# Causal attention with split values: two value products a block instead of three, row sums from the exp, and the rope's high parts on GpSimd

## What is computed

```python
q = (xn @ wq)                       # per head: 128 numbers without position, 64 with rope
ckv, k_pe = split(xn @ wkv_a)       # 64 latent numbers, 64 rope numbers, shared by the heads
ckv = ckv * rsqrt(mean(ckv**2) + eps) * kv_norm_scale
k_nope, v = split(ckv @ wkv_b)      # per head
scores = (q_nope . k_nope + rope(q_pe) . rope(k_pe)) * 192 ** -0.5, causal
s = concat_heads(softmax(scores) @ v) @ wo
g = silu(ffn(xn))                   # 256 -> 704 -> 256, ternary weights
out = x + s * g
```

## Time and profile before

| | |
|---|---|
| median of 3 runs | 1092.98 us (1091.6 to 1100.86) |
| the profiled execution | 1093.28 us, its span 1091.5 us |
| mean granted TensorE clock | 0.953 |
| busy of the span: PE / PEld | 971.0 us (89%) / 839.1 us (77%) |
| DVE / ACT / POOL | 739.6 us (68%) / 790.7 us (72%) / 716.4 us (66%) |
| DMA packets | 591978, 170.23 MB |
| the chain that ended last, by engine | PE 36%, POOL 17%, ACT 13%, issue 11%, DVE 8%, DMA 8%, SPq 6% |

### The profile page before, as it was taken

How to read it: one execution, slowest core, us unless ns; L and a number is a source line. 1 busy time by engine, 2 the same in 40 slices (tenths; PEclk the granted TensorE clock), 3 DMA queues, 4 the chain that set the end, 5 groups by cost and what they waited for, 6 DMA issues and landing times.

```text
span 1091.5 us, 26364 instructions
## 1 busy us (share of the span) xinstructions
PE 971.0 (89%) x10560; PEld 839.1 (77%) x10560; DVE 739.6 (68%) x1093; ACT 790.7 (72%) x1157; POOL 716.4 (66%) x514
## 2 busy tenths in 40 slices
PE   5648988999898979998989899979899997889998
PEld 5636877878787868786878787868787786777887
DVE  5747767777777767686778777877767785762134
ACT  1439887888788877888788878887888786663222
POOL 3657867696759685878487848784878576723231
PEclk7879998999999999998999999999989998899999
DMA  5019999999999989999999999998999999992001
GB/s 169 10 49 171 184 171 178 176 181 181 185 170 176 196 165 171 171 178 178 170 182 176 181 180 183 186 179 167 177 175 179 158 177 196 187 168 78 1 20 59
DMA packets 591978, 170.23 MB, mean 156 GB/s; under 512 B 574064, under 2 KB 585968, under 8 KB 591856
## 3 DMA queue, kind: packets, MB, share of 16 engines
...
## 4 chain that ended last, share of the span: by engine, by line
PE 36%; POOL 17%; ACT 13%; issue 11%; DVE 8%; DMA 8%; SPq 6%; ACTq 1%; POOLq 0%; DVEq 0%
PE s_ps L623 14%; PE s_ps L525 9%; POOL hl L1113 8%; ACT hl L729 6%; PE slot_ps L525 5%; POOL pe L1113 4%; ACT prob L806 4%; DMA pT<-hl 4%; SPq L468 3%; DVE part_max L945 3%; POOL q_swap L1113 3%; DVE hl L954 2%; PE o_ps L525 2%; PE o_ps L640 2%; ACT QB_hi L729 2%
## 5 line engine op out<-in xcount | busy, mean ns | idle before, releaser
L1113 POOL TENSOR_TENSOR hl<-prob,hl 128x1024 f16<-128x1024 f32 (+4 forms) x256 | 407.4, 1592 | 218.7 <-ACT hl L729 208.3
L806 ACT ACTIVATE prob<-s_ps,neg_max 128x1024 f32<-128x1024 f32 (+7 forms) x384 | 318.3, 863 | 113.7 <-DVE neg_max L948 80.3
L945 DVE TENSOR_REDUCE part_max<-s_ps 128x1 f32<-128x1024 f32 (+7 forms) x256 | 245.0, 986 | 152.5 <-PE s_ps L623 140.3
L729 ACT ACTIVATE hl<-prob 128x1024 f16<-128x1024 f32 (+7 forms) x384 | 296.4, 806 | 29.8 <-DMA pT<-hl 27.8
L639 PE MATMUL o_ps<-v,pT 128*128 128x65 f16 x2176 | 230.9, 194 | 5.3 <-DMA pT<-hl 3.9
L640 PE MATMUL o_ps<-v,pT 128*128 128x64 f16 x2176 | 231.3, 196 | 0.0
L641 PE MATMUL o_ps<-v,pT 128*128 128x65 f16 x2176 | 230.0, 193 | 0.0
L954 DVE TENSOR_TENSOR hl<-prob,hl 128x1024 f16<-128x1024 f32 (+3 forms) x128 | 170.6, 1333 | 73.8 <-ACT hl L729 72.4
L639 PEld LDWEIGHTS o_ps<-v,pT 128*128 128x128 f16 x2176 | 205.9, 97 | 6.4 <-DMA pT<-hl 4.6
L641 PEld LDWEIGHTS o_ps<-v,pT 128*128 128x128 f16 x2176 | 205.2, 100 | 0.0
L640 PEld LDWEIGHTS o_ps<-v,pT 128*128 128x128 f16 x2176 | 204.5, 98 | 0.0
(11 more groups left out here) (182 smaller groups left out, 1919.0 us busy)
## 6 DMA issues: line engine op xcount, KB each, us to landing
q_swap<-q_pe SPq DMA_DIRECT2D x128, 64.0 KB, 2.1
pT<-hl SPq DMA_TRANSPOSE x256, 5.1
...
```

What stands on the lines that cost most here:

```text
L729: return nc.scalar.activation(dst, src, ACT.Copy)
L806: nc.scalar.activation(prob_of(u, m), score_bank(u, m), ACT.Exp, bias=neg_max[:, r:r + 1]).then_inc(exp_done, 1)
L945: nc.vector.tensor_reduce(part_max[:, u % 2, m:m + 1], src, AX.X, ALU.max).then_inc(part_done, 1)
L1113: return lambda: nc.gpsimd.tensor_tensor(dst, a, b, op)
```

## The change

1. *Values.* v loses its column of ones and is 128 columns (high part, low part). A block takes two products: the probabilities' high half by all 128 columns, the low half by the first 64. The two output parts (2 heads, 2 tiles, 2 parts of 64 columns) fill the output bank.
2. *Row sums.* The exp accumulates its row (accum_out) into row_sum, one column for each part.
3. *normalise* on DVE: one add for the sums of parts 0 and 1, a copy of the second output part from the bank, the reciprocal, an add of the first part, then the product as before (now from SBUF). PE's next write to the bank waits for the first add of the parts (o_done) instead of the product (norm_done).
4. *Rope.* ACT keeps one copy of three (pe_b, now with two buffers), one unit later (k = 4, 6, 12, 14). POOL makes the high parts by a product with ones (A2hi, B2hi and so on), ahead of each low part. For the first pair's A DVE makes them. q_pe and q_swap have one buffer: ACT's copy of the next group's first query waits for the swap and rope.0 of the group before, and the swap for rope.2.
5. *Lists.* Jobs are laid out anew: units 0, 2 and 15 lose outP2b, outT3 and outP2a, the outputs come later, units 12 and 13 get some. The feed-forward's weights are loaded and scaled two units earlier, its scaling over three units; outT2 of the last pair goes to the tail.

```diff
-VW = 2 * LORA + 1
+VW = 2 * LORA
-JOBS_BEFORE = {0: ["outP2b"], 2: ["outT3"], 3: ["outP3a", "outP3b"]}
-JOBS_OWN = {0: ["qB2"], 1: ["qA1"], 2: ["qB1"], 5: ["wvo"], 6: ["outT0"], 7: ["outP0a"], 8: ["outP0b"], 10: ["outT1"],
-            11: ["outP1a", "outP1b"], 14: ["outT2"], 15: ["outP2a"]}
-JOBS_NEXT = {4: ["wqT", "wkvT"], 5: ["wabs"], 7: ["qA3"], 8: ["qB3"], 9: ["qA0"], 10: ["qB0"], 15: ["qA2"]}
+JOBS_BEFORE = {3: ["outP2a", "outP2b"], 4: ["outT3"], 5: ["outP3a"], 6: ["outP3b"]}
+JOBS_OWN = {0: ["qB2"], 1: ["qA1"], 2: ["qB1"], 7: ["wvo"], 8: ["outT0"], 11: ["outP0a", "outP0b"], 12: ["outT1"],
+            13: ["outP1a", "outP1b"], 14: ["outT2"]}
+JOBS_NEXT = {4: ["wqT"], 5: ["wkvT"], 6: ["wabs"], 7: ["qA3"], 8: ["qB3"], 9: ["qA0"], 10: ["qB0"], 15: ["qA2"]}
-FFN_COUNT = {8: 1, 9: 2, 10: 1, 12: 2, 13: 2, 14: 1, 15: 2}
+FFN_COUNT = {7: 1, 8: 1, 9: 2, 10: 2, 12: 1, 14: 2, 15: 2}
-POOL_NEXT = {1: ["wkvs"], 6: ["wpe_hi", "wpe_lo"], 9: rope(3)[:1], 10: rope(3)[1:], 11: ["A3lo", "B3lo"] + rope(0)[:1], 12: rope(0)[1:],
-             13: ["A0lo", "B0lo"]}
-POOL_OWN = {1: rope(2)[:1], 2: rope(2)[1:], 3: ["A2lo", "B2lo"] + rope(1)[:1], 4: rope(1)[1:], 5: ["A1lo", "B1lo"]}
-POOL_FFN = {6: ["up_zero", "up_scale_zero", "down_zero"], 8: ["up_scaled0", "up_scaled1"], 9: ["down_scaled"]}
-ROPE_HI_OWN, ROPE_HI_NEXT = {3: 2, 5: 1}, {11: 3, 13: 0}
+POOL_NEXT = {1: ["wkvs"], 6: ["wpe_hi", "wpe_lo"], 9: rope(3)[:1], 10: rope(3)[1:], 11: rope(0)[:1] + side("A", 3), 12: rope(0)[1:] + ["B3hi"],
+             13: ["B3lo"] + side("A", 0), 14: side("B", 0)}
+POOL_OWN = {1: rope(2)[:1], 2: rope(2)[1:], 3: rope(1)[:1] + side("A", 2), 4: rope(1)[1:] + ["B2hi"], 5: ["B2lo"] + side("A", 1), 6: side("B", 1)}
+POOL_FFN = {4: ["up_zero", "up_scale_zero", "down_zero"], 6: ["up_scaled0"], 7: ["up_scaled1"], 8: ["down_scaled"]}
+ROPE_B_OWN, ROPE_B_NEXT = {4: 2, 6: 1}, {12: 3, 14: 0}
...
-                if n >= 2:
-                    before = GROUP_ORDER[(n - 2) % NG], (n - 2) // NG
+                if n >= 1:
+                    before = GROUP_ORDER[(n - 1) % NG], (n - 1) // NG
                     sp.wait_ge(pool_done, POOL.after((f"rope{before[0]}.2", before[1])))
...
                 if m == 0 and head_of(u) == 0 and u >= 2:
-                    pe_eng.wait_ge(norm_done, u // 2)
+                    pe_eng.wait_ge(o_done, u)
...
-                    nc.tensor.matmul(whole, pT[:, b, :], v[:, kb, 0:LORA + 1], start=(m != 1 and b == 0), stop=False)
-                    nc.tensor.matmul(part, pT[:, b, :], v[:, kb, LORA + 1:VW], start=False, stop=False)
-                    last = nc.tensor.matmul(whole, pT[:, n + b, :], v[:, kb, 0:LORA + 1], start=False, stop=(m > 0 and b == n - 1))
+                    nc.tensor.matmul(whole, pT[:, b, :], v[:, kb, :], start=(m != 1 and b == 0), stop=False)
+                    last = nc.tensor.matmul(part, pT[:, n + b, :], v[:, kb, 0:LORA], start=False, stop=(m > 0 and b == n - 1))
...
-                    if n >= 2:
-                        before = GROUP_ORDER[(n - 2) % NG], (n - 2) // NG
-                        act.wait_ge(swapped, 64 * (n - 1))
+                    if n >= 1:
+                        before = GROUP_ORDER[(n - 1) % NG], (n - 1) // NG
+                        act.wait_ge(swapped, 64 * n)
                         act.wait_ge(pool_done, POOL.after((f"rope{before[0]}.0", before[1])))
...
-                copy(queries(Q_hi, 0, g)[0:ROPE, :], pe[0:ROPE, n % 2, :])
-                copy(pe_b[:], pe[ROPE:P, n % 2, :])
-                copy(queries(Q_hi, 1, g)[0:ROPE, :], pe[ROPE:P, n % 2, :]).then_inc(rope_hi, 1)
+                copy(pe_b[:, n % 2, :], pe[ROPE:P, n % 2, :]).then_inc(rope_b, 1)
...
-                nc.scalar.activation(prob_of(u, m), score_bank(u, m), ACT.Exp, bias=neg_max[:, r:r + 1]).then_inc(exp_done, 1)
+                nc.scalar.activation(prob_of(u, m), score_bank(u, m), ACT.Exp, bias=neg_max[:, r:r + 1],
+                                     accum_out=row_sum[:, u % (2 * DEN), m:m + 1]).then_inc(exp_done, 1)
...
+                nc.vector.tensor_tensor(sums[:, :, 1:2], sums[:, :, 0:1], sums[:, :, 1:2], ALU.add).then_inc(sum_done, 1)
                 dve.wait_ge(pv_done, scores_through(u))
-                nc.vector.reciprocal(r, o[:, :, :, LORA]).then_inc(recip_done, 1)
+                nc.vector.tensor_copy(o_sum[:], o[:, :, :, 1, :]).then_inc(o_done, 1)
+                dve.wait_ge(sum_done, n + 1)
+                nc.vector.reciprocal(r, sums[:, :, 1:3]).then_inc(recip_done, 1)
+                dve.wait_ge(o_done, 2 * n + 1)
+                nc.vector.tensor_tensor(o_sum[:], o[:, :, :, 0, :], o_sum[:], ALU.add).then_inc(o_done, 1)
...
+                if name.endswith("hi"):
+                    free = ((scores_ready, queries_free(head, g, pair)),) if pair > 0 else ()
+                    added = ((rope_b, n + 1),) if head else ()
+                    run((name, pair), tt(hi, src, ones[0:ROPE, :].to_broadcast([ROPE, BANK]), ALU.mult), *free, *added)
```

More of the change, by code:

```diff
@@ L125 @@
 KIND.update({"up": SPLIT, "down": SPLIT})
-JOBS_BEFORE = {0: ["outP2b"], 2: ["outT3"], 3: ["outP3a", "outP3b"]}
-JOBS_OWN = {0: ["qB2"], 1: ["qA1"], 2: ["qB1"], 5: ["wvo"], 6: ["outT0"], 7: ["outP0a"], 8: ["outP0b"], 10: ["outT1"],
-            11: ["outP1a", "outP1b"], 14: ["outT2"], 15: ["outP2a"]}
-JOBS_NEXT = {4: ["wqT", "wkvT"], 5: ["wabs"], 7: ["qA3"], 8: ["qB3"], 9: ["qA0"], 10: ["qB0"], 15: ["qA2"]}
+JOBS_BEFORE = {3: ["outP2a", "outP2b"], 4: ["outT3"], 5: ["outP3a"], 6: ["outP3b"]}
+JOBS_OWN = {0: ["qB2"], 1: ["qA1"], 2: ["qB1"], 7: ["wvo"], 8: ["outT0"], 11: ["outP0a", "outP0b"], 12: ["outT1"],
+            13: ["outP1a", "outP1b"], 14: ["outT2"]}
+JOBS_NEXT = {4: ["wqT"], 5: ["wkvT"], 6: ["wabs"], 7: ["qA3"], 8: ["qB3"], 9: ["qA0"], 10: ["qB0"], 15: ["qA2"]}
 JOBS_FIRST = {0: ["qA2"]}
-FFN_COUNT = {8: 1, 9: 2, 10: 1, 12: 2, 13: 2, 14: 1, 15: 2}
+FFN_COUNT = {7: 1, 8: 1, 9: 2, 10: 2, 12: 1, 14: 2, 15: 2}
 EARLY = {PU * PAIRS - 1: (0, 2), PU * PAIRS: (2, 4)}
-OUT_LAST = {0: ("outP2a", PAIRS - 1), 1: ("outP2b", PAIRS - 1), 5: ("outT3", PAIRS - 1), 7: ("outP3a", PAIRS - 1), 8: ("outP3b", PAIRS - 1)}
+OUT_LAST = {j: (name, PAIRS - 1) for j, name in ((0, "outT2"), (1, "outP2a"), (2, "outP2b"), (5, "outT3"), (7, "outP3a"), (8, "outP3b"))}
 def jobs_at(u):
@@ L249, in mla_gated_ffn_kernel @@
         sinT = ab("sinT", [P, S])
-        q_pe = ab("q_pe", [P, 2, BANK])
-        q_swap = ab("q_swap", [P, 2, BANK])
+        q_pe = ab("q_pe", [P, BANK])
+        q_swap = ab("q_swap", [P, BANK])
         pe = ab("pe", [P, 2, BANK])
-        pe_b = ab("pe_b", [LORA, BANK])
+        pe_b = ab("pe_b", [LORA, 2, BANK])
         wq_sb = ab("wq_sb", [P, KE, QW])
@@ L319, in mla_gated_ffn_kernel @@
         rinv = ab("rinv", [P, 2, 4])
+        row_sum = ab("row_sum", [P, 2 * DEN, 3])
+        o_sum = ab("o_sum", [P, 2, 2, LORA])
         attn.close()
@@ L453, in swap @@
                     a, b = slice(i * half, (i + 1) * half), slice((i ^ 1) * half, (i ^ 1) * half + half)
-                    sp.dma_start(q_swap[a, n % 2, :], q_pe[b, n % 2, :]).then_inc(swapped, 16)
+                    sp.dma_start(q_swap[a, :], q_pe[b, :]).then_inc(swapped, 16)
             def turn_first(u):
@@ L488, in _ @@
                     load(pair + 1)
-                if pair < PAIRS - 1 and k == 7:
+                if pair < PAIRS - 1 and k == 8:
                     sp.wait_ge(slot_ready, after("ready", ("wvo", pair)))
                     load_wo(pair + 1)
-                if pair == PAIRS - 1 and k == 6:
+                if pair == PAIRS - 1 and k == 4:
                     load_ffn()
@@ L842, in _ @@
                     pair, k = divmod(u, PU)
-                    if k in ROPE_HI_OWN:
-                        rope_high(ROPE_HI_OWN[k], pair)
-                    if k in ROPE_HI_NEXT and pair < PAIRS - 1:
-                        rope_high(ROPE_HI_NEXT[k], pair + 1)
+                    if k in ROPE_B_OWN:
+                        rope_of_b(ROPE_B_OWN[k], pair)
+                    if k in ROPE_B_NEXT and pair < PAIRS - 1:
+                        rope_of_b(ROPE_B_NEXT[k], pair + 1)
                     prob_high(u, 1)
@@ L1016, in split_first @@
                 hi, lo = queries(Q_hi, 0, g)[0:ROPE, :], queries(Q_lo, 0, g)[0:ROPE, :]
-                dve.wait_ge(rope_hi, group_no(g, 0) + 1)
+                dve.wait_ge(pool_done, POOL.after((f"rope{g}.2", 0)))
+                then_wait(nc.vector.tensor_copy(hi, src))
                 nc.vector.tensor_tensor(lo, src, f32(hi), ALU.subtract).then_inc(queries_split, 1)
@@ L1135, in rope_step @@
                     done = ((queries_split, n - 1),) if 2 <= n < 4 else ()
-                    run((name, pair), tt(turned, q_pe[:, n % 2, :], cosT[:, query_cols(g)], ALU.mult), (hi_done, after("hi", (f"qB{g}", pair))),
+                    run((name, pair), tt(turned, q_pe[:], cosT[:, query_cols(g)], ALU.mult), (hi_done, after("hi", (f"qB{g}", pair))),
                         (tables_loaded[g], 32), *done)
```

(11 more changed lines are left out.)

48 lines of the change are left out of this document (27 added, 21 removed).

## The result

The changed kernel takes 1106.18 us (median of 8 runs, 1101.32 to 1112.24) against 1092.93 us before (8 runs beside them): a ratio of 1.0102, 95% interval [1.008, 1.0124]. The forecast was 1067, with 1036 to 1104 as its range. Sign and size are both wrong. The granted TensorE clock of the profiled executions is the same, 0.955 against 0.953.

What follows compares the result with a forecast made beforehand. PE was taken to pace k = 15 to 2 and 7 to 10, waits the rope stretches, SP's queue the floor (105.9 us a pair). Pairs from 112 to 108.9 give 25 less, setup 1: 1093.3 to about 1067, range 1036 to 1104.

Steps and rivals of the forecast that it cites:

- Values: Value products on PE: 88 ns a block, 4.6 less; 10 us of PE, half counted, 5 us; ends 14 gained, 9 lost.
- Row sums: 384 exps on ACT also write a sum: 0.19 us each, bounds 0 and 365 ns, 9.1 us of ACT a pair.
- slower: the sum's read on ACT: Rival, chance 0.14: sum reads after 384 exps cost up to 0.365 us each; every 0.1 us costs 26 us; up to 1113.
- Rope on ACT: At k = 3 to 6 and 11 to 14: eight copies a pair go, 5.0 us, and the rope.2 wait, 3.5 a pair.
- Rope on POOL: Eight high products a pair at 1.12 us, 9.0 us of POOL; cost 0, up to 2.5 us per rope stretch.
- normalise: On DVE: 1.0 us more, 64 times; hidden at five or six of eight places, late at two: 1.8 us a pair.
- One buffer for q_pe: ACT's q_pe copy waits for the previous group's swap: 0.8 us, twice a pair, 1.6 us.
- Lists: Jobs leave the PE-bound stretches k = 15 to 2 and 7 to 10: 1.8 and 1.0 us less; tail gets 0.4.
- The sum: Stretch times for a pair, from k = 15: 26.5, 26.6, 25.9, 26.2; together 105.2, taken as 108.9 us.
- POOL becomes the bound: Rival, chance 0.18: in the rope stretches POOL's products and DVE's low halves slow each other; each stretch 1.1 us longer; about 1093.
- four named signs of failure: ACT over 100 us a pair; SP waiting for POOL's low halves; ACT wait before q_pe over 1 us; PE waiting for bank.
- The floor: Rival, chance 0.20: SP's queue of transposes and swaps needs 105.9 us a pair, reached in every pair; 49 less, 1044.

Runs made afterwards that it cites:

- n: Kernel before with new lists, exps' row sums, three 64-column value products a block, normalise without copy and add, old rope part: 1081.8 us, ratio 0.9894.
- j: Kernel before with the new job lists, exps also accumulating row sums that nothing reads: 1083.03 us, ratio 0.9917.
- c: Kernel before, old lists, with exps accumulating row sums that nothing reads: 1096.74 us, ratio 1.0036.
- a: The change with the rope's high parts copied on ACT again and POOL without its high products: 1097.68 us, ratio 1.0019.
- l: Kernel before with new lists, low rope products a unit later, two q_pe buffers, high parts copied on ACT, old value part: 1081.64 us, ratio 0.9900.
- i: Kernel before with new lists and the change's rope part but two q_pe buffers; values, sums and normalise old: 1086.6 us, ratio 0.9940.
- e: The change with two q_pe buffers, the sum of value parts held in o_tiles for room: 1102.24 us, ratio 1.0047.
- k: The change with high parts copied on ACT, normalise free of operations with two SBUF inputs, and two q_pe buffers: 1079.94 us, ratio 0.9874.
- f: Kernel before with new lists and the change's value part (two products, exps' sums, changed normalise), old rope part: 1123.07 us, ratio 1.023.

## Why the prediction was wrong, by its own steps

- **Values.** 88 ns a block, ends 80 and 101: measured 85, 57 for the product of 128 columns and 28 for that of 64. Right in direction, and more. The 5 us that I counted were not seen: no run has the products alone, and n, beside j, gains 2.5 us, within the noise.
- **Row sums.** 0.19 us: measured 0.197. The rival "slower: the sum's read on ACT" has the right sign of the whole by luck and the wrong place: it needed 0.29 us a sum, and c gives 4 us for all of them, j 7 to 9. Its weight, 26 us for each 0.1 us of the sum, is not borne out either: 0.197 would make 51.
- **Rope on ACT.** Right where it looked: the wait for rope.2 went, and k = 3, 5, 11 and 13 take 6.13, 6.91, 6.41 and 6.96 us, all under the 8 that I named. My sums for the rope stretches, 26.6 and 26.2, were measured as 25.3 and 26.4. But I let the waits vanish, and they moved: ACT's wait for transposes, which "stays" by my text, grew from 27.8 to 52.7 us, and the units behind lost more than these gained.
- **Rope on POOL.** The products at 1.12 us are right (1.06 and 1.13); "Cost 0, with up to 2.5 us per rope stretch" took the lower end. It cost 1.1 a pair by a, 0.5 by l against i. I let POOL be late because "at k = 7 and 8 POOL catches up", and did not look at what stands in POOL's list there: at k = 6 wpe_lo, on which PE's job of k = 7 waits.
- **normalise.** This is the step that failed most. "1.0 us, 64 times" was 1.78, since I priced the product from SBUF by its row from PSUM, where it never waits for POOL, and the add of sums by the reciprocal: 0.47 and 0.31 us more than priced, on the mean, and what is more is the wait for POOL's instruction. And "hidden at five or six" of eight places rested on DVE's idle time in one unit each. In the sum for k = 7 to 10 I weighed PE (24.1) and ACT (25.9) and had no term for DVE, which came to 26.8 of 30.6 in the pair shown. The slack that I gave PE at the bank was not there either: 11.3 us of waits. With the rope part in, mending the SBUF pairs gives 11 us, without it 29.
- **One buffer for q_pe.** 0.8 us twice a pair: the one at 543.95 is 1.59, the longest 3.2, since the swap stands behind two loads on SP. Worth 6 us by e, nothing by i.
- **Lists.** Right: 16 to 18 us alone, where 1.8 and 1.0 us a pair less the tail's 0.4 come to 22.
- **The sum.** By stretch, 15 to 2: 26.5, measured 29.9; 3 to 6: 26.6 and 25.3; 7 to 10: 25.9 and 31.8; 11 to 14: 26.2 and 26.4. The stretches that the change was aimed at are right to 1.3 us; what is wrong is that I let it cost almost nothing in the stretches bound by PE. Of the 39 us between forecast and result, mending POOL's products, normalise and the q_pe buffer (k) gives back 25. The other 14 are gains that I counted and that k does not show; which of them fail, and why, is open.
- **The rivals.** "POOL becomes the bound" (1093) named the contention and came nearer than my forecast, but put it on POOL's new products. Three of the four named signs of failure came true: SP waited 131.6 us for POOL's low halves (91.7 before; but a, which is faster, has 139.9), ACT before q_pe, PE for the bank. The fourth did not: ACT was busy for 734 us in the main stage, 92 a pair and not over 100. The floor is neither reached nor refuted: no kernel here comes under 109.7 us a pair, where it is 105.9.

The parts do not add up from one side: the lists give 16 to 18; on them the rope part costs 9, the value part 41, but both together 28. Beside f, the rope part takes back 14 us of what the value part costs. It takes copies off ACT in the stretches where the exps wait for DVE, which would explain it; no run separates that.

No kernel here is faster than the one with the lists alone, 1077.9 us, 1.5% under the kernel before and 2.5% under the change.
